# A causal mask added to attention scores by a second product on TensorE instead of inside VectorE's maximum

## The reference, cut to what matters

```
q, k, v = heads of 8 columns              # 16 heads, 512 tokens
s = q @ k.T * scale                       # 512 x 512 per head
s = where(tril, s, -1e9)
p = softmax(s)
out = p @ v
```

## Time and profile before

| | |
|---|---|
| median of 3 runs | 3166.05 us (3158.64 to 3183.53) |
| the profiled execution | 3194.17 us, its span 3192.4 us |
| PE busy | 2670.9 us, 84% |
| DVE busy | 1758.7 us, 55% |
| ACT busy | 1299.2 us, 41% |
| mean granted TensorE clock | 0.820 of 2.4 GHz |

### The profile page before, as it was taken

How to read it: one execution, slowest core, us unless ns; L and a number is a source line. 1 busy time by engine, 2 the same in 40 slices (tenths; PEclk the granted TensorE clock), 3 DMA queues, 4 the chain that set the end, 5 groups by cost and what they waited for, 6 DMA issues and landing times.

```text
span 3192.4 us, 39656 instructions
## 1 busy us (share of the span) xinstructions
PE 2670.9 (84%) x13585; PEld 1357.3 (43%) x13585; DVE 1758.7 (55%) x4863; ACT 1299.2 (41%) x3060; POOL 605.6 (19%) x849
## 2 busy tenths in 40 slices
PE   4888998889988887888758988987899888888885
PEld 2233335434553585244423333353345446742363
DVE  5535446654564597633465444485356547776154
ACT  1445632353324442563424556214532344435741
POOL 0330001221101483000012200012201127720000
PEclk7688988678887998768768888977798789988776
DMA  5100001200000001100011000022001000011000
GB/s 168 23 1 1 1 1 33 50 11 21 24 24 1 1 8 41 48 1 31 18 48 22 1 1 1 1 46 47 1 20 34 14 1 1 29 46 22 1 1 7
DMA packets 37787, 67.51 MB, mean 21 GB/s; under 512 B 4873, under 2 KB 30345, under 8 KB 35722
## 3 DMA queue, kind: packets, MB, share of 16 engines
q1 hardware_dynamic: 37010, 63.69, 7.8%
q10 hardware_dynamic: 576, 1.29, 0.1%
HBM read 44.45 MB, written 1.05 MB: 14 GB/s over the span
## 4 chain that ended last, share of the span: by engine, by line
PE 64%; DVE 17%; ACT 8%; issue 6%; SPq 1%; POOL 1%; DMA 1%; ACTq 0%; POOLq 0%; DVEq 0%
PE psum L567 5%; PE psum L989 4%; PE psum L2149 4%; PE psum L1000 3%; PE psum L557 3%; DVE floor_s L2248 3%; PE psum L973 2%; PE psum L1524 2%; PE psum L815 2%; PE psum L740 2%; PE psum L1354 2%; PE psum L539 2%; PE psum L1816 2%; DVE mx_s L705 2%; PE psum L1802 2%
## 5 line engine op out<-in xcount | busy, mean ns | idle before, releaser
L641 ACT ACTIVATE PT_s<-psum 128x512 f32<-128x512 f32 (+3 forms) x768 | 341.9, 496 | 283.7 <-PE psum L557 282.2
L386 POOL TENSOR_SCALAR ve<-mv 128x4 f32<-128x4 f32 x48 | 13.6, 282 | 1649.3 <-DVE mv L376 1649.1
L539 PE MATMUL psum<-KS_s,QS_s 48*128 48x512 bf16 (+3 forms) x768 | 214.4, 416 | 113.8 <-DMA QS_s<-parts_s 56.3
L2175 POOL TENSOR_TENSOR buffer<-sim_s 128x1024 f32<-128x1024 f32 x128 | 271.8, 2138 | 176.1 <-DVE floor_s L2248 94.3
L702 DVE CUSTOM_DVE_ANT_0 rest_s<-psum,packed_early 128x128 f32<-128x128 f32 (+3 forms) x512 | 225.8, 487 | 89.6 <-PE psum L539 86.7
L567 PE MATMUL psum<-PT_s,vaug 128*9 128x512 f32 (+3 forms) x1536 | 199.7, 599 | 52.9 <-POOL PT_s L675 35.9
L557 PE MATMUL psum<-QS_s,KS_s 51*128 51x512 bf16 (+3 forms) x768 | 208.7, 391 | 34.7 <-ACT PT_s L641 21.1
L675 POOL TENSOR_SCALAR_AFFINE_SELECT PT_s<-PT_s 128x128 f32<-128x128 f32 x512 | 148.7, 301 | 392.2 <-ACT PT_s L641 387.6
L2208 ACT ACTIVATE above_s<-buffer,below_s 128x1024 f32<-128x1024 f32 x128 | 145.4, 1149 | 135.6 <-PE psum L2149 91.7
L1037 ACT ACTIVATE PT_s<-psum 128x512 f32<-128x512 f32 (+1 forms) x224 | 121.1, 592 | 170.0 <-PE psum L991 169.9
L705 DVE TENSOR_REDUCE mx_s<-psum 128x1 f32<-128x512 f32 x256 | 159.9, 682 | 50.0 <-PE psum L539 49.4
(11 more groups left out here) (441 smaller groups left out, 5132.4 us busy)
## 6 DMA issues: line engine op xcount, KB each, us to landing
buffer<-packed_experts SPq DMA_DIRECT2D x36, 384.0 KB, 3.5
KS_s<-parts_s SPq DMA_DIRECT2D x192, 48.0 KB
QS_s<-parts_s SPq DMA_DIRECT2D x192, 48.0 KB
buffer<-packed_moe SPq DMA_DIRECT2D x4, 2048.0 KB, 8.0
buffer<-packed_cross SPq DMA_DIRECT2D x4, 2048.0 KB, 7.8
buffer<-packed_product SPq DMA_DIRECT2D x4, 1024.0 KB, 4.8
packed_early<-packed_early SPq DMA_DIRECT2D x1, 2654.0 KB
QS_s<-nmT_s SPq DMA_DIRECT2D x144, 4.0 KB
```

The lines of the kernel that those rows point to most:

```text
L539: pe.matmul(bank[n % 4][:, 0:n_keys], QS[stack(h), h // 2, j * P:(j + 1) * P], KS[stack(h), h // 2, 0:n_keys], start=True, stop=True, tile ...
L641: a.activation(PT[:, u // 4 % 2, i, q0_of(c):T], bank[u % 3][:, q0_of(c):T], ACT.Exp, scale=scale).then_inc(exp_done.sem, 1)
L2175: g.tensor_tensor(fs[:, n % 2], m[:, 0, :].unsqueeze(2).to_broadcast([P, NK, NK]), m[:, 1, :].unsqueeze(1).to_broadcast([P, NK, NK]), ALU. ...
```

## The change

The constants get a bfloat16 identity and the 128 x 128 bfloat16 block with 0 on and below the diagonal and -1e30 above it. After each causal score product, a second product (identity as weights, mask block as moving data, whole array, 128 columns) adds the mask to the diagonal block of the same bank, and its end now tells VectorE that the score is ready. VectorE's instruction with two inputs, a full-size output (`junk`) and an accumulated maximum gives way to a plain reduction over the bank, and the wait that protected `junk` goes. The unmasked case keeps its instructions.

```diff
+    c["ident16"] = np.eye(P, dtype=np.float32).astype(mybir.dt.np(BF16))
+    c["causal16"] = mask[:, T - P:].astype(mybir.dt.np(BF16))
...
-    junk = rest
...
-                pe.matmul(bank[n % 4][:, 0:n_keys], QS[stack(h), h // 2, j * P:(j + 1) * P], KS[stack(h), h // 2, 0:n_keys],
-                          start=True, stop=True, tile_position=(64 * (h % 2), 0)).then_inc(ring_ready.sem, 1)
+                mm = pe.matmul(bank[n % 4][:, 0:n_keys], QS[stack(h), h // 2, j * P:(j + 1) * P], KS[stack(h), h // 2, 0:n_keys],
+                               start=True, stop=not causal, tile_position=(64 * (h % 2), 0), skip_group_check=True)
+                if causal:
+                    mm = pe.matmul(bank[n % 4][:, j * P:(j + 1) * P], s.w["ident16"][:], s.w["causal16"][:], start=False, stop=True,
+                                   skip_group_check=True)
+                mm.then_inc(ring_ready.sem, 1)
...
-                if causal:
-                    w = (j + 1) * P
-                    if u >= 2:
-                        v.wait_ge(*scores_read(u - 1))
-                    v.tensor_tensor_reduce(junk[:, u % 2, 0:w], bank[n % 4][:, 0:w], s.w["causal"][:, T - w:T], 1.0, -3e38,
-                                           ALU.add, ALU.max, mx[:, j, h:h + 1]).then_inc(scores_read.sem, 1)
-                else:
-                    v.tensor_reduce(mx[:, j, h:h + 1], bank[n % 4][:], AX_X, ALU.max).then_inc(scores_read.sem, 1)
+                v.tensor_reduce(mx[:, j, h:h + 1], bank[n % 4][:, 0:(j + 1) * P if causal else T], AX_X, ALU.max).then_inc(scores_read.sem, 1)
```

## The result

The changed kernel takes 3288.9 us (median of 4 runs, 3286.6 to 3293.5), the kernel before 3171.7 in the same comparison: ratio 1.037, 95% interval 1.033 to 1.042, or 117 us more. The forecast was 110 us more, 3276 us for the median, in a range of 3210 to 3335. The profiled execution after has a span of 3285.3 us, only 93 us over that of before, because the profiled execution of before was a long one of its kind (22 us over this median).

What follows compares the result with a forecast made beforehand. The prediction took TensorE as the bound, busy 84% of the span with 64% of the chain. Its terms, 99 + 6 + 6 - 1 = +110 us on a median of 3166, gave 3276 us, range 3210 to 3335.

Steps and rivals of the forecast that it cites:

- The mechanism and its price: On TensorE's list, a mask product with passages out of and back to the half array: 0.25 us at 2.4 GHz, 0.35 at 1.2.
- The overlap of neighbouring scores: Scores in different halves run side by side; losing this costs 4.4 us a stretch, 26 us in six.
- Rival A: TensorE loads the mask product's weights early, so only its columns remain: 0 to +15 us, 3166 to 3181; chance 0.07.
- The six stretches: Causal-score stretches except the first and that from 1588 us: 132 us more on TensorE's list, of which 99 show.
- the credit of 80 bursts: Score bursts already followed by a whole-array product need no new passage there: 0.2 us each, 16 us off.
- one share, three quarters: PE and issue hold about three quarters of the chain in the six stretches, so 132 x 0.75 = 99 us show.
- The first stretch: Causal scores at the start without a second stream; the last 32 become bound by TensorE's list: +6 us.
- The stretch from 1588 us: Causal scores where VectorE is fuller; 22 us of additions mostly fall into TensorE's idle time: 0 to 22, taken as +6.
- The start: Two more 32 KB constants loaded by SP are covered by VectorE's own work: nothing; without cover 1 us, once.
- the saving of 7 us: VectorE's plain maximum saves 0.01 to 0.02 us a score, 7 us in all, mostly beside TensorE's work; 1 us counted.
- Rival B: Added products hold TensorE's clock high in the stretches' low-clock time, making the kernel faster: 3130 us; chance 0.05.
- Rival C: No idle time absorbs the additions; all 132 us shows, plus 6 and 22 elsewhere: +160 us, 3326; chance 0.2.

Runs made afterwards that it cites:

- the second experiment: Mask product in the score's own half of the array, with VectorE's old instruction, against the kernel before: 3167.9 us, ratio 0.9955.
- the first experiment: Whole-array mask product added but VectorE keeping its old instruction with mask, junk output and wait, against the kernel before: 3290.2 us, ratio 1.034.
- the fifth experiment: Whole-array product with a single moving column after each causal score, VectorE's old instruction, against the kernel before: 3273.9 us, ratio 1.031.

## Why the prediction was right, and what in it was not

*The mechanism and its price.* Leaving the half for the mask product costs 0.10 to 0.11 us at both clocks, the return 0.11. Over all the places in the changed kernel's trace where score and mask product follow each other, the medians are 0.105 us to leave and 0.108 to return at 2.4 GHz, 0.110 and 0.114 at 1.2. With columns that is 0.05 + 0.10 + 0.11 = 0.26 us at 2.4 GHz and 0.11 + 0.11 + 0.11 = 0.33 at 1.2, for which I had 0.25 and 0.35. The runs with the product in the half and with one column, with the starts in their timelines, show that the whole-array product between half-array scores is the cause, by its passages, and not the number of products, their columns, the later signal or VectorE. The overlap of neighbouring scores goes with the passages in every run, so its share (26 of 132 us in the forecast) has no run of its own. The Trainium skill, TensorEngine Tiling (Array Packing), Key Properties, has TensorE drained when the tiling mode changes, and not when only the tile does. The trace agrees on both, with 0.10 to 0.11 us at a change, and in the second experiment no such time between a score and a product in the halves.

*Rival A* (the passages vanish) is refuted for the whole-array product and is exactly what happens inside the half: no time, as priced.

*The six stretches* were put at +99 us and measured +96. What stands behind the sum can be counted. The 859 changes of kind are 608 more than before, not the 768 of two for each of 384 products: 80 pairs fewer, as many as the credit of 80 bursts had. TensorE's busy time in the six grew by 132.6 us, beside 132 forecast for its list, and its idle time fell from 43.2 to 6.7. By an estimate from the medians above, 608 passages are 66 us and the columns 37; the 30 us that are left are lost overlap (26 in the forecast) and the lower clock together, which no run divides. So part of the agreement is luck, since the clock's fall was no term of the sum.

The agreement of the total also hides two errors of opposite sign, and it is one of two single executions, of which that of before was long. I applied one share, three quarters, to all. The two stretches beside whole-array products of the other stream (from 553.7 and 2124.5) grew by 9 and 11 us: TensorE's busy time grew there by 14 and 15, for the credit is largest there, and 5 and 4 us of idle time took the rest. The four with exponentials grew by 14, 19, 22 and 22 (their lengths before were 57.0, 51.3, 48.7 and 48.0), where 16 each was forecast. In those, first, the idle time was filled almost to nothing, so ScalarE's and GpSimd's waits went off the chain; second, the granted clock fell, from 0.65, 0.57, 0.82 and 0.68 to 0.62, 0.52, 0.62 and 0.52. I had kept the clock of before and named as a risk only that it could rise.

*The first stretch*: +6, as forecast, at 0.76 us for a score of 512 columns with its mask where I had written 0.78. *The stretch from 1588 us*: +6 forecast, -1 measured; all of TensorE's addition fell into its idle time, which went from 29 to 14 us, and VectorE remained the fuller engine, just (53.8 us beside 52.1). *The start*: the late loads start at 15.98 us, as before; nothing, as forecast.

*VectorE.* The saving in busy time was wrong in sign: 1758.7 became 1767.4 us. Its instruction is no dearer: with the product taken away, VectorE's busy time is 1748.9 us, 10 us under the kernel before, and with the product it is 1767.4, 9 us under the 1776.7 of the first experiment. So the saving of 7 us was about right as a price. What raises the busy time is the product, by 18 us with either instruction. That an instruction that waits overlaps its neighbour less, so that the tail of each counts, would explain it; this is argued, not shown.

*Rival B* (the clock pays it back) was wrong for the change; for the half product it fits what was seen, though no run proves it (last section). *Rival C* (+160) had too much: idle time did fill.

*Slips.* 64 / 3 x 0.2 is 4.3, not 4.4, and the high end by its own rule would be 3338, not 3335; neither changes the forecast.

## What to carry to other kernels

Before a small product is added to a stream of products on part of the array, look at what it costs to pass from part to whole and back, which a trace shows as the distance between starts less the columns: here 0.2 us for a pair of passages, two to four times the product itself. The same work, cut so that it stays in the part (even as two products instead of one), took no more time than the kernel before. And an instruction moved from an engine with slack to the one that bounds needs a reason in its own stage: VectorE waited for TensorE at this very line.

## What the runs showed of the hardware that was not expected

The granted clock fell where passages were added and rose where the same products were added without them. The view is busy time by stretch, of one of the stretches with exponentials (629.8 to 681.1 us in the kernel before, PEclk 0.57). With passages and one column, the fifth experiment above:

```profile
645.10:710.20 65.10, 64.31 (x305) 22.94 (x305) 36.13 (x156) 24.00 (x53) 13.89 (x45) 0.50 0.13 22
```

With one product in the half, and with two:

```profile
617.60:660.50 42.90, 35.72 (x305) 15.22 (x307) 32.62 (x151) 19.86 (x52) 13.38 (x45) 0.86 0.20 34
```

```profile
616.80:660.10 43.30, 37.27 (x365) 18.71 (x367) 32.53 (x151) 20.04 (x52) 13.33 (x45) 0.89 0.20 34
```

PE is busy for 99% of the first by its records, and the clock is at the low level throughout. In the third it has more matmuls in less time, busy for 86%, and has a mean of 0.89. The same view of all four stretches with exponentials, each from the start of its first maximum to the end of its last; the time at 1.2 GHz is worked out from the granted clock, as in rival B:

| kernel | four stretches, us | of it at 1.2 GHz |
|---|---|---|
| before | 208 | 135 |
| plain maximum alone | 196 | 98 |
| one half product | 188 | 60 |
| the same, repeated | 186 | 51 |
| two half products, VectorE's old instruction | 183 | 34 |
| exact mask in halves | 187 | 50 |
| the change | 284 | 243 |
| one column, whole array | 277 | 261 |

Each row is one profiled execution. The two of one half product agree stretch by stretch, 0.92, 0.84, 0.89 and 0.71 beside 0.97, 0.84, 0.89 and 0.75, and the change's 0.62, 0.52, 0.62 and 0.52 lie beside 0.56, 0.50, 0.62 and 0.52 of the first experiment; the step between the two kinds is far larger than either difference. The step from the kernel before is less sure: the plain maximum alone adds no columns and already has 98 us instead of 135. The reading that fits is that products added in the half partly paid for themselves, and that passages went with a lower clock for everything around them, beside their own time; it is not proved. How the 117 us divide between the two is not settled: no run held the clock fixed.
